# Softmax normalisation of a vision-transformer layer: whole-image Vector instructions, a third buffer, and a new order of the matmuls

## The chip, the core and the metric

The kernel runs on one core of one Trainium2 chip. The metric is the device time of one execution, in microseconds (us). It was timed three times before the change: 1443.85, 1444.19 and 1445.03 us.

Engines as the profile names them: PE is TensorE's matmuls, PEld its weight loads, DVE is VectorE, ACT is ScalarE, POOL is GpSimd, SP is SyncE, whose queue (SPq) here only issues DMAs.

## The reference

A patch embedding, one attention block with fake-quantised operands, and a gated feed-forward block with quantised weights. The change is in the attention block, of 64 images with 197 tokens, width 192, 12 heads of 64:

```python
def fake_quant(q, s, z):
    zr = ste_round(z)
    return s * (jnp.clip(ste_round(q / s) + zr, 0.0, 15.0) - zr)
...
qkv = fake_quant(x, sx1, zx1) @ fake_quant(ww1, sw1, zw1).T
q, k, v = map(split_heads, jnp.split(qkv, 3, axis=-1))
dots = jnp.einsum('bhnd,bhmd->bhnm', fake_quant(q, sq, zq), fake_quant(k, sk, zk)) * scale
a = jax.nn.softmax(dots, axis=-1)
out = jnp.einsum('bhnm,bhmd->bhnd', fake_quant(a, sa, za), fake_quant(v, sv, zv))
return fake_quant(out, sx2, zx2) @ fake_quant(ww2, sw2, zw2).T + bb2
```

So each image needs 12 score matrices of 197x197, their exponentials, the sum of each query's exponentials, a division, a rounding to int16, a clip to 0..15, and a product with the values.

## The kernel before

Three stages run one after the other: the embedding (18 packs of tiles, until some 230 us of the profiled span), the attention (one image after another, until some 1067 us) and the feed-forward (49 pairs of 128-row tiles and a rest). The engines are written out by hand, each in its own block, and meet through semaphores. Each engine works strictly in the order of its block; what orders the attention stage are `SLOTS` (the table of matmul pieces) and the order of the statements in each `image_step`.

**Layout.** Scores are kept transposed: keys on the partitions, queries along the free axis. The 197 keys of an image are two blocks, `TOK`: 128 keys and 69 keys (t = 0, 1). A unit u = 0..5 of an image is four heads (group g = u // 2) of one key block (t = u % 2): 4 x 197 = 788 columns.

**Pieces.** `image_step(b, par)` runs once per image b, with 6 slots. In slot u the tensor engine does the first piece of `SLOTS[u]`, then the scores of the next unit (L1149, four matmuls, called S below), then the sums of the unit before (L1161, called Z: a 32-column stationary operand with one non-zero column gathers the sum over keys of exp; four fp32 matmuls, recorded as eight), then the rest of the slot's pieces. The pieces, with the image that they serve as an offset to b:

- xt (L1093): transposes of the next image's input, which ACT copies to `xT` (L500)
- qk 0..5 (L1101): four matmuls each, which ACT rounds to `qki` (L504) and DVE clips to `qkb`, one clip for q and one for k
- v 0..3 (L1108): two matmuls each, rounded to `vi` by ACT (L513), clipped to `vb` by DVE
- o 0..2 (L1118, L1120): the product of probabilities and values of four heads, PV below: eight matmuls with 64 stationary columns, of which even heads write partitions 0 to 63 and odd heads 64 to 127; ACT rounds the result to `oi` (L525)
- y 0..1 (L1126): the output projection, from `ob`, which DVE clips from `oi`

Three PSUM banks (5, 6, 7) take the pieces in turn, so a piece waits until ACT has read the piece three places before it. Two pairs of banks take the scores, one pair for each t.

**Softmax.** ACT exponentiates a unit from PSUM into `ex` (L544), a ring of 12 units (2 images). When image b-1's last Z is done, DVE transposes the 12 x 197 sums (L877), takes reciprocals (L887) and transposes back to `zinv` (L906). SP writes them to DRAM in three DMAs (`z_row`, L415) and reads them back spread over all 128 partitions in three DMAs (`zb`, L420), one for each group of four heads, each with a semaphore of its own. DVE multiplies one unit of `ex` with its group of `zb` into int16 `pi` (L913, called TT below), 11 units behind the scores, and clips the unit to bf16 `pT` (L766 through `clip`, called clip P) one unit later:

```python
dve.wait_ge(s_zb[g], 16 * (image + 1))
dve.wait_ge(s_exp, U - TT_LAG + 1)
wait(dve, s_pb, U - TT_LAG - 1)
v.tensor_tensor(pi[0:r, t, :, 0:N], ex[0:r, w % U1 + U1 * ((par + w // U1) % 2), :, :], zb[0:r, g, :, :],
                ALU.mult).then_inc(s_pi, 1)
```

A PV piece of group k waits for both clips of its group, `pe.wait_ge(s_pb, 2 * G + 2)`.

Of the kernel before, what the change touches and what calls it, by code (L numbers as in the profile page):

```python
# [5 lines left out]
def vit_tower_kernel(nc, xt, w_tok, tok_b, cls_tok, w1t, w2t, bb2, quant, w_in_t, g_in, w_out_t, g_out,  # L6
# [10 lines left out]
    ALU = mybir.AluOpType  # L17
# [3 lines left out]
    B, N, D = out.shape  # L21
# [14 lines left out]
    with ctx:  # L36
# [42 lines left out]
        big = sb("big", [128, NR + NF + ND + PACK * KC * 128], fp32)  # L79
# [3 lines left out]
        xring = big[:, NR + NF + ND:].rearrange("p (a b) -> p a b", a=PACK)  # L83
        hb = sb("hb", [128, 2, PACK, D], fp32)
        hp = sb("hp", [128, 2, PACK, D], fp32)
# [5 lines left out]
        xi = sb("xi", [128, PACK, D], i16)  # L91
        xb = sb("xb", [128, 2, PACK, D], bf16)
# [3 lines left out]
        stage_i = sb("stage_i", [128, 2 * 3 * INNER], i16)  # L96
# [22 lines left out]
        pi = sb("pi", [128, 2, 4, N + 1], i16)  # L119
        pT = sb("pT", [128, 3, 2, 4, N + 1], bf16)  # L120
# [43 lines left out]
        s_zb = [sem(f"softmax_inverse_spread_{g}") for g in range(3)]  # L164
        s_zrow = [sem(f"softmax_inverse_stored_{g}") for g in range(3)]
# [119 lines left out]
        TT_LAG, CLIP_LAG = 11, 12  # L285
# [69 lines left out]
        def over_images(eng, step):  # L355


            for b in range(-1, 5):
                step(b, b % 2)
            with eng.Fori(0, (B - 8) // 2) as i:  # L360
                step(2 * i + 5, 1)
                step(2 * i + 6, 0)
            for b in range(B - 3, B + 3):
                step(b, b % 2)
# [10 lines left out]
        def _(sp):  # L375
# [29 lines left out]
            def image_step(b, par):  # L405
# [10 lines left out]
                if has_unit(b, -U1):  # L416
                    for g in range(3):
                        wait_apart(sp, s_zrow[g], 16 * b)
                        wait_apart(sp, s_pi, 6 * (b - 2) + 2 * g + 2)
                        sp.dma_start(zb[:, g, :, :].rearrange("p h n -> p (h n)"),  # L420
                                     z_row[g, :, :].rearrange("h n -> (h n)").partition_broadcast(128))\
                          .then_inc(s_zb[g], 16)
# [19 lines left out]
        def _(act):  # L442
# [92 lines left out]
            def image_step(b, par):  # L535
                n = 0
                for u in range(U1):
                    U = U1 * b + u
                    if exists(b, 0):
                        r = TOK[u % 2][1]  # L540
                        act.wait_ge(s_scores, U + 1)
                        wait(act, s_pi, U - 11)

                        act.activation(ex[0:r, U1 * par + u, :, :].rearrange("p (a h) n -> p a h n", a=2),  # L544
                                       psum[0:r, 2 * (u % 2):2 * (u % 2) + 2, 0:2 * N]
# [80 lines left out]
        def _(pool):  # L626
# [45 lines left out]
            def image_step(b, par):  # L672
# [44 lines left out]
        def _(dve):  # L717
# [555 lines left out]
```

## Time and profile before

| | us |
|---|---|
| median of 3 runs (lowest, highest) | 1444.19 (1443.85, 1445.03) |
| the profiled execution | 1445.15 |
| its span, first to last instruction | 1443.2 |
| DVE busy / PE busy / ACT busy in it | 1209.8 / 1218.4 / 990.7 |

The span is what the trace shows; the profiled execution's own time is 2.0 us longer than it. Busy time of PE is that of overlapping, modelled matmul records, so PE is read by the distance from the start of one group of matmuls to the start of the next, and by what it waited for.

### The profile page before, as it was taken

The numbers are of one execution on the slowest core, as the hardware profiler recorded it, in microseconds if no ns is written. First come the engines' busy times: TensorE is split into PE (matmuls) and PEld (weight loads), VectorE is DVE, ScalarE is ACT, GpSimd is POOL, SyncE is SP. The second block draws the span as 40 slices with busy tenths as digits, with TensorE's granted clock in tenths as the row PEclk, the third lists the DMA queues.
The fourth block names the chain that finished last, engine by engine and source line by source line (L and its number), as shares of the span: only waits on it lengthen the run. The fifth ranks groups of instructions, "written<-read, shape, count | busy, mean of one in ns | idle before, by whom it ended". The sixth has DMA issues, their size and how long they took to land.

```text
span 1443.2 us, 40676 instructions
## 1 busy us (share of the span) xinstructions
PE 1218.4 (84%) x11806; PEld 761.2 (53%) x11806; DVE 1209.8 (84%) x2868; ACT 990.7 (69%) x2005; POOL 457.1 (32%) x540
## 2 busy tenths in 40 slices
PE   5999992999999999999999999999846766767676
PEld 5999991445555555555555555555523333333343
DVE  4566782269999999999999999999978999999996
ACT  0000002568888888888888888888817888888886
POOL 7344541001111111111111111111126666666664
PEclk9999995569999999999999999999956787777765
DMA  6999972124444444444444444444532222222222
GB/s 246 267 281 276 299 246 64 44 76 117 119 120 120 120 120 120 120 120 120 120 119 121 120 119 119 117 120 117 126 75 61 83 82 82 82 82 86 83 73 69
DMA packets 142650, 182.38 MB, mean 126 GB/s; under 512 B 40528, under 2 KB 104784, under 8 KB 142288
## 3 DMA queue, kind: packets, MB, share of 16 engines
q1 hardware_dynamic: 71472, 134.72, 31.7%
q10 hardware_dynamic: 55776, 37.45, 8.8%
q0 software_dynamic: 15360, 9.70, 5.7%
q8 instruction: 20, 0.33, 0.1%
q14 instruction: 22, 0.18, 0.0%
HBM read 147.31 MB, written 34.50 MB: 126 GB/s over the span
## 4 chain that ended last, share of the span: by engine, by line
PE 74%; DVE 9%; issue 7%; ACT 5%; ACTq 2%; DMA 1%; DVEq 0%; SPq 0%; POOL 0%
PE psum L1044 13%; PE psum L1161 13%; PE psum L1101 12%; PE psum L1149 8%; PE psum L1108 7%; PE psum L1183 5%; PE psum L1126 5%; PE psum L1118 4%; PE psum L1120 2%; DVE big L1002 2%; ACT xT L500 2%; PE psum L1093 1%; PE psum L1204 1%; DVE oo L1019 1%; ACT big L574 1%
## 5 line engine op out<-in xcount | busy, mean ns | idle before, releaser
L913 DVE TENSOR_TENSOR pi<-big 128x788 int16<-128x788 f32 (+1 forms) x384 | 370.4, 965 | 0.0
L677 POOL DMA_DIRECT2D h_res<-att x128 | 118.1, 959 | 724.1 <-ACT att L520 722.4
L544 ACT ACTIVATE big<-psum 128x788 f32<-128x788 f32 (+1 forms) x384 | 314.8, 820 | 2.9 <-DVE pi L913 2.9
L1101 PE MATMUL psum<-xT,w1b 96*128 96x197 bf16 x1536 | 196.3, 259 | 43.3 <-ACT xT L500 43.3
L504 ACT ACTIVATE qki<-psum 128x394 int16<-128x394 f32 x384 | 179.1, 498 | 59.2 <-PE psum L1101 54.7
L1161 PE MATMUL psum<-big,sa_hot 128*32 128x197 f32 (+1 forms) x3072 | 216.0, 355 | 0.0
L1044 PE MATMUL psum<-big 128*128 128x192 f32 (+1 forms) x1200 | 197.3, 330 | 19.3 <-DMA big<-xt 17.3
L1044 PEld LDWEIGHTS psum<-big 128*128 128x128 f32 (+1 forms) x1200 | 195.4, 190 | 20.3 <-DVE big L722 17.2
L766 DVE TENSOR_SCALAR pT<-pi,lo,hi 128x788 bf16<-128x788 int16 (+1 forms) x384 | 185.3, 483 | 22.3
L1101 PEld LDWEIGHTS psum<-xT,w1b 96*128 96x128 bf16 x1536 | 124.6, 100 | 124.9 <-issue 65.8
L1183 PE MATMUL psum<-winb,zT 96*128 96x512 bf16 (+1 forms) x396 | 150.3, 548 | 34.8 <-DVE big L1002 34.2
L500 ACT ACT_TABLE_LOAD x1 | 1.3, 1283 | 238.6 <-issue 238.6
L1149 PE MATMUL psum<-qkb 64*128 64x197 bf16 (+1 forms) x1536 | 140.4, 263 | 2.6 <-DVE qkb L766 1.2
L766 DVE TENSOR_SCALAR qkb<-qki,lo,hi 128x1182 bf16<-128x1182 int16 x128 | 75.9, 593 | 77.9 <-ACT qki L504 77.9
L711 POOL TENSOR_TENSOR big<-big,goutb 128x512 f32<-128x512 f32 (+1 forms) x99 | 124.0, 1274 | 47.6 <-DVE big L1002 47.6
L513 ACT ACTIVATE vi<-psum 128x384 int16<-128x384 f32 (+1 forms) x256 | 117.9, 485 | 30.8 <-PE psum L1108 29.5
L1108 PE MATMUL psum<-w1b,xT 96*128 96x384 bf16 (+1 forms) x512 | 110.7, 341 | 0.0
L525 ACT ACTIVATE oi<-psum 128x394 int16<-128x394 f32 x192 | 97.2, 506 | 14.2 <-PE psum L1120 14.2
L1183 PEld LDWEIGHTS psum<-winb,zT 96*128 96x128 bf16 (+1 forms) x396 | 45.8, 126 | 113.1 <-issue 66.6
L1118 PE MATMUL psum<-pT,vb 128*64 128x197 bf16 x768 | 89.6, 264 | 12.4 <-issue 7.4
L1213 PE MATMUL psum<-woutb,yT 128*128 128x192 bf16 (+1 forms) x396 | 51.3, 285 | 56.7 <-ACT yT L566 56.7
L1161 PEld LDWEIGHTS psum<-big,sa_hot 128*32 128x32 f32 (+1 forms) x3072 | 61.7, 110 | 63.5 <-issue 26.5
(105 smaller groups left out, 1966.1 us busy)
## 6 DMA issues: line engine op xcount, KB each, us to landing
big<-z_row SPq DMA_DIRECT2D x192, 394.0 KB, 3.8
big<-xt SPq DMA_DIRECT2D x98, 384.0 KB, 4.3
tin<-h_res SPq DMA_DIRECT2D x49, 192.0 KB, 2.4
tres<-h_res ACTq DMA_DIRECT2D x49, 192.0 KB, 2.5
out<-oo ACTq DMA_DIRECT2D x49, 192.0 KB, 2.6
h_res<-hp ACTq DMA_DIRECT2D x96, 96.0 KB, 3.8
h_res<-att POOLq DMA_DIRECT2D x64, 96.0 KB, 3.5
x_int<-xb ACTq DMA_DIRECT2D x96, 48.0 KB, 3.9
```

The lines of the kernel that those rows point to most:

```text
L504: act.activation(qki[:, 2 * k:2 * k + 2, :], psum[:, bank, 0:2 * N] .rearrange("p (c n) -> p c n", c=2), ACT.Copy, scale=factor[F_Q if k < ...
L544: act.activation(ex[0:r, U1 * par + u, :, :].rearrange("p (a h) n -> p a h n", a=2), psum[0:r, 2 * (u % 2):2 * (u % 2) + 2, 0:2 * N] .rear ...
L711: g.tensor_tensor(yg[0:r, oth, a, :], yy[0:r, a, :], goutb[0:r, :], ALU.mult)\
L766: return v.tensor_scalar(dst, src, lo[0:r, which:which + 1], hi[0:r, which:which + 1], ALU.max, ALU.min)
L913: v.tensor_tensor(pi[0:r, t, :, 0:N], ex[0:r, w % U1 + U1 * ((par + w // U1) % 2), :, :], zb[0:r, g, :, :], ALU.mult).then_inc(s_pi, 1)
L1044: last = mm(psum[p0:p0 + r, s, 0:D], xring[:, s, c * 128 + p0:c * 128 + p0 + r], weight_of(cls, c), start=(c == 0), stop=(c == KC - 1))
L1101: last = mm(psum[:, bank, j * N:(j + 1) * N], w1b[:, c, ch:ch + 128], xT[:, c, :], start=(c == 0), stop=(c == 1))
L1108: last = mm(psum[0:r, bank, 0:W], xT[:, c, t0:t0 + r], w1b[:, c, 2 * INNER + half * W:2 * INNER + (half + 1) * W], start=(c == 0), stop=(c ...
L1118: mm(dst, vb[:, ip, 0, head * DH:(head + 1) * DH], pT[:, k, 0, j, 0:N], start=True, stop=False)
L1149: last = mm(psum[0:r, 2 * (w % 2) + i % 2, (i // 2) * N:(i // 2 + 1) * N], qkb[po:po + DH, ip, 6 + c, t0:t0 + r], qkb[po:po + DH, ip, c, 0:N],
L1161: last = mm(psum[32 * j:32 * j + 32, 4, 0:N], sa_hot[0:r, w // 2, :], ex[0:r, U1 * ip + w, j, :], start=(w == 0), stop=(w == 5))
L1183: last = mm(psum[0:r, 2 * a + half, :], zT3[:, oth, a, c, 0:r], winb[:, c, half * HID:(half + 1) * HID], start=(c == 0), stop=(c == 1))
```

## The change

1. **DVE works by key block.** One TT and one clip P per image and key block, over all 12 heads (2364 columns), so two of each per image in place of six of each. `pi`, `pT`, `zb` and `ex` are laid out for that: `ex` is a ring of three images, `zb` and `pT` hold two images, `vb` three. `zb` has one semaphore, and a TT waits for all three of its DMAs.
2. **A new order on DVE**, for image step b: clip `vb`, clip P of image b-3 block 1, the three small steps on the sums, TT of image b-2 block 0, clip q, clip P block 0, clip k, clip `ob`, TT of image b-2 block 1.
3. **A new `SLOTS`.** All PV pieces belong to image b-3 and stand first in slots 1, 2 and 3; the input transposes stand at the end of slot 0, and the first qk pieces come after the PV piece, S and Z of slot 1.
4. **PV matmuls alternate column halves** in program order: head 0 and head 1 for the first key block, then both for the second.
5. `hb`, `hp`, `xi`, `xb`, `stage_i` move into the shared buffer `big` (they are used only before the attention). The loop over images is unrolled six times instead of twice (9 rounds instead of 28).

The core of the diff:

```diff
-        ex = big[:, 0:NEX].rearrange("p (u h n) -> p u h n", u=12, h=4)
-        zb = big[:, NEX:NEX + 12 * N].rearrange("p (g h n) -> p g h n", g=3, h=4)
+        ex = big[:, 0:6 * HN].rearrange("p (i t h n) -> p i t h n", i=3, t=2, h=HEADS)
+        zb = big[:, 6 * HN:8 * HN].rearrange("p (i h n) -> p i h n", i=2, h=HEADS)
...
-        SLOTS = [[("v", 3, 0), ("o", 2, -3), ("xt", 0, 1)],
-                 [("qk", 0, 1), ("qk", 1, 1)],
-                 [("o", 0, -2), ("qk", 2, 1), ("v", 0, 1)],
-                 [("qk", 3, 1), ("qk", 4, 1), ("qk", 5, 1)],
-                 [("o", 1, -2), ("y", 0, -3)],
-                 [("y", 1, -3), ("v", 1, 1), ("v", 2, 1)]]
+        SLOTS = [[("v", 3, 0), ("xt", 0, 1)],
+                 [("o", 0, -3), ("qk", 0, 1), ("qk", 1, 1)],
+                 [("o", 1, -3), ("qk", 2, 1), ("qk", 3, 1)],
+                 [("o", 2, -3), ("qk", 4, 1), ("qk", 5, 1)],
+                 [("v", 0, 1), ("v", 1, 1)],
+                 [("v", 2, 1), ("y", 0, -3), ("y", 1, -3)]]
...
+                    wait_apart(sp, s_zb, 48 * (b - 1))
                     for g in range(3):
-                        wait_apart(sp, s_zb[g], 16 * (b - 1))
-                        sp.dma_start(z_row[g, :, :], zinv[g:128:32, 0:N]).then_inc(s_zrow[g], 16)
...
+                        sp.dma_start(z_row[g, :, :], zinv[g:128:32, 0:N]).then_inc(s_zrow, 16)
+                    wait_apart(sp, s_zrow, 48 * b)
+                    wait_apart(sp, s_pi, 2 * b - 4)
                     for g in range(3):
...
+                def clip_probs(image, ip, t):
+                    r = TOK[t][1]
+                    dve.wait_ge(s_pi, 2 * image + t + 1)
+                    wait(dve, full["o"], 3 * (image - 1))
+                    clip(pT[0:r, ip, t, :, 0:N], pi[0:r, t, :, 0:N], None, r, ZA).then_inc(s_pb, 1)
+
+                def normalise(image, ip, it, t):
+                    r = TOK[t][1]
+                    dve.wait_ge(s_zb, 48 * (image + 1))
+                    dve.wait_ge(s_exp, U1 * (image + 1))
+                    wait(dve, s_pb, 2 * image + t - 1)
+                    v.tensor_tensor(pi[0:r, t, :, 0:N], ex[0:r, it, t, :, :], zb[0:r, ip, :, :],
+                                    ALU.mult).then_inc(s_pi, 1)
...
-                    G = 3 * im + k
-                    pe.wait_ge(s_pb, 2 * G + 2)
+                    it = (tri + d) % 3
+                    pe.wait_ge(s_pb, 2 * im + 2)
                     pe.wait_ge(s_vb, im + 1)
...
+                    for c in range(2):
+                        for t, r in ((0, 128), (1, R1)):
+                            for i in range(2):
+                                head, j = 4 * k + 2 * c + i, 4 * k + ORD.index(2 * c + i)
+                                last = mm(psum[i * DH:(i + 1) * DH, bank, c * N:(c + 1) * N],
+                                          vb[0:r, it, t, head * DH:(head + 1) * DH], pT[0:r, ip, t, j, 0:N],
+                                          start=(t == 0), stop=(t == 1))
```

What it moves on DVE, in a steady image. Before, from the transpose of the sums on (L913 is TT, L766 with `pT` is clip P):

```order
L877 STREAM_TRANSPOSE zt<-psum 128x224
L766 TENSOR_SCALAR pT<-pi,lo,hi 69x4x197
L887 RECIPROCAL zti<-zt 128x7x3
...
L766 TENSOR_SCALAR vb<-vi,lo,hi 128x1536
L906 STREAM_TRANSPOSE zinv<-zti 128x224
...
L913 TENSOR_TENSOR pi<-big 128x4x197
...
L766 TENSOR_SCALAR pT<-pi,lo,hi 128x4x197
...
L913 TENSOR_TENSOR pi<-big 69x4x197
L766 TENSOR_SCALAR pT<-pi,lo,hi 69x4x197
```

Now, the whole image (L888 is TT, L771 with `big<-pi` is clip P, since `pT` lies in `big`):

```order
L771 TENSOR_SCALAR vb<-vi,lo,hi 128x1536
L771 TENSOR_SCALAR big<-pi,lo,hi 69x12x197
L906 STREAM_TRANSPOSE zt<-psum 128x224
L909 RECIPROCAL zti<-zt 128x7x3
L912 STREAM_TRANSPOSE zinv<-zti 128x224
L888 TENSOR_TENSOR pi<-big 128x12x197
L771 TENSOR_SCALAR qkb<-qki,lo,hi 128x6x197
L771 TENSOR_SCALAR big<-pi,lo,hi 128x12x197
L771 TENSOR_SCALAR qkb<-qki,lo,hi 128x6x197
L771 TENSOR_SCALAR ob<-oi,lo,hi 128x6x197
L888 TENSOR_TENSOR pi<-big 69x12x197
```

The second TT is now the last instruction of an image step, and its clip the second of the next one.

What it moves on PE, around the input transposes. Before, the first qk piece follows them directly:

```order
L1093 MATMUL psum<-ident,xq 96x69
L1101 MATMUL psum<-xT,w1b 128x197 [waits xt_read,v_read]
L1101 MATMUL psum<-xT,w1b 128x197 x3
L1149 MATMUL psum<-qkb 128x197 [waits exp_done]
L1149 MATMUL psum<-qkb 128x197 x3
L1161 MATMUL psum<-big,sa_hot 32x197 [waits softmax_sum_turned,exp_done]
L1161 MATMUL psum<-big,sa_hot 32x197 x3
```

Now (L1105 transposes, L1131 PV, L1161 S, L1173 Z, L1113 qk):

```order
L1105 MATMUL psum<-ident,xq 96x69
L1131 MATMUL psum<-big,vb 64x197 [waits v_quantised,probs_quantised,v_read]
L1131 MATMUL psum<-big,vb 64x197 x7
L1161 MATMUL psum<-qkb 128x197 [waits exp_done]
L1161 MATMUL psum<-qkb 128x197 x3
L1173 MATMUL psum<-big,sa_hot 32x197 [waits softmax_sum_turned,exp_done]
L1173 MATMUL psum<-big,sa_hot 32x197 x3
L1113 MATMUL psum<-xT,w1b 128x197 [waits xt_read,v_read]
L1113 MATMUL psum<-xT,w1b 128x197 x3
```

Between the transposes and the first qk piece there now stand a PV piece, S and Z, and that PV piece is the one that waits for the clip of the second key block.

## Rows read from the trace of the kernel before

**Rows 1.** The page: busy time, and the chain that ended last.

```profile
PE 1218.4 (84%) x11806; PEld 761.2 (53%) x11806; DVE 1209.8 (84%) x2868; ACT 990.7 (69%) x2005; POOL 457.1 (32%) x540
PE 74%; DVE 9%; issue 7%; ACT 5%; ACTq 2%; DMA 1%; DVEq 0%; SPq 0%; POOL 0%
```

**Rows 2.** Windows: length, busy PE, PEld, DVE, ACT, POOL; PEclk, DMA share, GB/s.

```profile
290.00:310.00 20.00, 19.32 (x149) 9.00 (x147) 12.76 (x22) 12.38 (x24) 0.00 (x0) 0.50 0.25 69
310.00:330.00 20.00, 19.25 (x209) 10.97 (x202) 14.61 (x25) 14.55 (x31) 3.14 (x4) 0.82 0.35 83
700.00:724.28 24.28, 22.83 (x291) 12.93 (x289) 22.41 (x40) 21.47 (x45) 3.70 (x4) 1.00 0.45 119
319.50:1023.40 703.90, 661.85 (x8356) 374.85 (x8353) 649.78 (x1103) 622.74 (x1277) 107.29 (x116) 1.00 0.48 119
```

**Rows 3.** Waits, 342.2 to 1023.4 us: waited in total, times, longest.

```profile
PE psum L1101 <- ACT xT L500: 37.8, 56, 0.8
DVE qkb L766 <- ACT qki L504: 25.7, 112, 0.4
```

**Rows 4.** Timeline of PE, one image: start us, us, what.

```profile
701.57 0.86 PE L1101 MATMUL psum<-xT,w1b 96*128 96x197 bf16 x8
...
707.86 0.39 PE L1093 MATMUL psum<-ident,xq 128*96 128x128 bf16 x4
708.93 0.52 PE L1101 MATMUL psum<-xT,w1b 96*128 96x197 bf16 x4 [0.68 <-ACT xT L500]
709.38 0.34 PE L1149 MATMUL psum<-qkb 64*128 64x197 bf16 x4
709.66 0.54 PE L1161 MATMUL psum<-big,sa_hot 128*32 128x197 f32 x8
710.13 0.52 PE L1101 MATMUL psum<-xT,w1b 96*128 96x197 bf16 x4
710.58 0.28 PE L1118 MATMUL psum<-pT,vb 128*64 128x197 bf16 x2
710.69 0.26 PE L1120 MATMUL psum<-pT,vb 69*64 69x197 bf16 x2
...
711.05 0.36 PE L1149 MATMUL psum<-qkb 64*69 64x197 bf16 x4
711.34 0.54 PE L1161 MATMUL psum<-big,sa_hot 69*32 69x197 f32 x8
```

**Rows 5.** Timeline of ACT, same stretch.

```profile
701.73 1.28 ACT L504 ACTIVATE qki<-psum 128x394 int16<-128x394 f32 x3
```

**Rows 6.** Timeline of DVE, same stretch.

```profile
703.05 0.59 DVE L766 TENSOR_SCALAR qkb<-qki,lo,hi 128x1182 bf16<-128x1182 int16 x1 [0.26 <-ACT qki L504]
703.55 0.97 DVE L913 TENSOR_TENSOR pi<-big 69x788 int16<-69x788 f32 x1
704.56 0.48 DVE L766 TENSOR_SCALAR pT<-pi,lo,hi 69x788 bf16<-69x788 int16 x1
...
707.53 0.42 DVE L877 STREAM_TRANSPOSE zt<-psum 128x224 f32<-128x224 f32 x1
...
708.43 0.57 DVE L766 TENSOR_SCALAR vb<-vi,lo,hi 128x1536 bf16<-128x1536 int16 x1
708.92 0.40 DVE L906 STREAM_TRANSPOSE zinv<-zti 128x224 f32<-128x224 f32 x1
```

**Rows 7.** Timeline of DVE before the attention: fp32 TENSOR_TENSOR of other lengths.

```profile
15.38 1.63 DVE L722 TENSOR_TENSOR big<-big 128x1152 f32<-128x1152 f32 x1
...
24.84 0.36 DVE L776 TENSOR_TENSOR hb<-psum,tokb 128x192 f32<-128x192 f32 x1 [0.42 <-PE psum L1044]
```

**Rows 8.** Timeline of SP's queue, same image: issues of the reciprocals' DMAs.

```profile
709.49 1.69 SPq L415 DMA_DIRECT2D z_row<-zinv  x3
```

**Rows 9.** The tensor `z_row`: its DMAs, and the time from issue to landing.

```profile
L420 SPq DMA_DIRECT2D big<-z_row x192: 319/330/448, 269.8 to 1052.7; - x192
DMA to landing us min/median/max: 3.4/3.8/5.3
```

More of the change, by code:

```diff
@@ L82, in vit_tower_kernel @@
         wmix = big[:, NR + NF:NR + NF + ND].rearrange("p (a b c) -> p a b c", a=2, b=2)
[L83 to L85 removed]
+        xring = big[:, o_x:o_h].rearrange("p (a b) -> p a b", a=PACK)
+        hb, hp = [big[:, o_h + k * NH:o_h + (k + 1) * NH].rearrange("p (a b c) -> p a b c", a=2, b=PACK)
+                  for k in range(2)]
         st = sb("st", [128, PACK, 6], fp32)
@@ L163, in vit_tower_kernel @@
         s_zinv = sem("softmax_inverse_ready")
-        s_zb = [sem(f"softmax_inverse_spread_{g}") for g in range(3)]
-        s_zrow = [sem(f"softmax_inverse_stored_{g}") for g in range(3)]
+        s_zb = sem("softmax_inverse_spread")
+        s_zrow = sem("softmax_inverse_stored")
         s_pi = sem("probs_int16_ready")
@@ L284, in vit_tower_kernel @@
         U1 = 6
-        TT_LAG, CLIP_LAG = 11, 12
         def has_unit(b, u):
@@ L358, in over_images @@
             for b in range(-1, 5):
[L359 to L364, printed above, removed]
+                step(b, b % 2, b % 3)
+            rounds = (B - 8) // 6
+            with eng.Fori(0, rounds) as i:
+                for j in range(6):
+                    step(6 * i + 5 + j, (5 + j) % 2, (5 + j) % 3)
+            for b in range(5 + 6 * rounds, B + 3):
+                step(b, b % 2, b % 3)
         def dst_rows(dram, y, x, half, along_x):
@@ new lines, in clip_qk @@
+                def clip_qk(half):
+                    dve.wait_ge(evac["qk"], 6 * (b + 1) + 3 * (half + 1))
+                    wait(dve, s_scores, 6 * b)
+                    clip(qkb[:, nxt, 6 * half:6 * half + 6, 0:N], qki[:, 6 * half:6 * half + 6, :], None,
+                         128, (ZQ, ZK)[half]).then_inc(s_qkb, 1)
+                if has_unit(b, -U1):
+                    dve.wait_ge(evac["v"], 4 * b)
+                    wait(dve, full["o"], 3 * (b - 3))
+                    clip(vb[:, (tri + 2) % 3, :, :], vi[:, nxt, :, :], None, 128, ZV).then_inc(s_vb, 1)
@@ new lines, in image_step @@
+                if has_unit(b, -3 * U1):
+                    clip_probs(b - 3, nxt, 1)
+                if has_unit(b, -U1):
+                    dve.wait_ge(s_zsum, b)
+                    wait(dve, s_zti, b - 1)
+                    v.transpose(zt[:, :, :].rearrange("p a b -> p (a b)"), psum[:, 4, 0:NZ]).then_inc(s_zt, 1)
+                    dve.wait_ge(s_zt, b)
+                    wait(dve, s_zinv, b - 1)
+                    v.reciprocal(zti[:, :, 0:3], zt[:, :, 0:3]).then_inc(s_zti, 1)
+                    dve.wait_ge(s_zti, b)
+                    wait(dve, s_zrow, 48 * (b - 1))
+                    v.transpose(zinv[:, :], zti[:, :, :].rearrange("p a b -> p (a b)")).then_inc(s_zinv, 1)
@@ new lines, in image_step @@
+                if has_unit(b, -2 * U1):
+                    normalise(b - 2, par, (tri + 1) % 3, 0)
+                if exists(b, 1):
+                    clip_qk(0)
+                if has_unit(b, -2 * U1):
+                    clip_probs(b - 2, par, 0)
+                if exists(b, 1):
+                    clip_qk(1)
+                if has_unit(b, -3 * U1):
+                    dve.wait_ge(evac["o"], 3 * b - 6)
+                    wait(dve, full["y"], 2 * b - 6)
+                    clip(ob[:, :, 0:N], oi[:, nxt, :, :], None, 128, ZX2).then_inc(s_ob, 1)
```

110 lines of the change are left out of this document (32 added, 78 removed).

## Prediction

> **What bounds the kernel now.** I read four views, from coarse to fine. The page's busy times and chain [rows 1] show PE and DVE both at 84% of the span, and PE on 74% of the chain that ended last. Neither says which of the two sets the pace, so the attention stage is read by itself. The windows [rows 2] show 703.90 us of it at a granted clock of 1.00 (2.4 GHz). One turn of the image loop, two images, is 24.28 us there, so an image takes 12.14 us and the stretch holds 703.90 / 12.14 = 58 images. In the turn DVE is busy 22.41 us and ACT 21.47 of 24.28.
>
> The waits [rows 3] name the pace: PE waits 56 times in 56 images for ACT's copy of the transposed input, 37.8 / 56 = 0.68 us each. DVE waits 112 times for ACT's rounding of q and k, 25.7 / 56 = 0.46 us per image, and ACT there waits for PE's products. So DVE follows PE with 0.46 us to spare, and PE is the bound. In the timeline of PE [rows 4] the reader is to see that groups start right behind each other (the next starts before the last one's modelled end), except at 708.93, where qk stands 1.07 us behind the transposes with 0.68 us idle.
>
> **What the groups cost, from start to next start** [rows 4]: a PV piece 711.05 - 710.58 = 0.47, S 0.28 (128 keys) or 0.29 (69 keys), Z 0.47, two qk pieces in a row 0.86 less the overlap of 0.07 = 0.79.
>
> **PE after the change.** Between transposes and the first qk piece now lie PV, S and Z: 0.47 + 0.28 + 0.47 = 1.22 us, more than the 0.68 waited. That wait leaves. Every piece is still there, and the switches between the shapes of group are as many as before, so PE's own need is 12.14 - 0.68 = 11.46 us an image.
>
> **DVE after the change.** TT: 788 elements take 0.97 us [rows 6], 192 take 0.36 [rows 7], so 0.61 / 596 = 1.02 ns an element, and 2364 take 0.97 + 1576 x 1.02 = 2.58; I take 2.61, since the shorter one reads PSUM and its slope may be a little low. Bounds: 2.58, and 3.34 at the rate of the other row of its kind (1152 in 1.63 us, beside adds of POOL) [rows 7]; three old ones would be 2.91. I take the low end because the 788-element row is this very instruction. Clip P: 788 take 0.48 and 1182 take 0.59 [rows 6], 0.27 ns an element, so 2364 take about 0.90. Bounds: 0.67 by the slope to the 1536-element clip (0.57), and three old ones, 1.45. By these, DVE saves per image 6 x 0.97 - 2 x 2.61 = 0.60 and 6 x 0.48 - 2 x 0.90 = 1.08 us, 1.7 together: it needs about 10 us an image and is far from being the bound by its sum. That saving is worth nothing in itself, since DVE already waited.
>
> **But the order closes a ring.** The first PV piece of step b waits for both clips of image b-3, and the second is the second DVE instruction of step b. In front of it on DVE stand, in order: clip k (which waits for ACT's reading of qk piece 5 of the step before), clip `ob`, the second TT, clip `vb`. And qk piece 5 stands behind that step's three PV pieces. So one image can't be shorter than this ring:
>
> - PE, start of PV 0 to end of qk 5: 3 PV 1.41, S 0.28 + 0.29 + 0.28, 3 Z 1.41, two qk pairs 1.58, and the third to its end 0.86: 6.11
> - ACT: qk ends at 701.57 + 0.86 = 702.43, its reading at 701.73 + 1.28 = 703.01 [rows 4, 5]: 0.58; and 0.04, since ACT is still reading qk 4 when qk 5 ends
> - to DVE 0.04 (703.05) [rows 6]
> - DVE: clip k to the next start 0.50 (703.05 to 703.55), clip `ob` (as many elements) the same 0.50, TT 2.61 less the 0.08 by which an independent instruction starts early = 2.53, clip `vb` 0.49 (708.43 to 708.92), clip P whole 0.90: 4.92
> - back to PE 0.07 (an estimate, of the size of the 0.04 from ACT to DVE)
>
> The sum is 11.76 us. It is above PE's 11.46, so the ring binds, and PE stands 0.3 us before the first PV piece. The gain is 12.14 - 11.76 = 0.38 us an image, over 58 images 22.0 us.
>
> **The rest.** Four images before 319.5 us run at a clock of 0.50 (1.2 GHz) and 96% busy PE [rows 2]; groups are longer there and DVE is only 64% busy, so PE binds and 0.68 leaves each time: 2.7 us. The third image of `ex` and of `vb` only frees waits that did not occur. The DMAs of the reciprocals stay six per image (three stores, three reads), but all three reads now wait for all three stores. Stores start 0.17 behind `zinv` (708.92 + 0.40) and are issued by 711.18 [rows 6, 8]; with an estimated 1.5 to land, then three issues of 0.33 and up to 5.3 for the reads to land [rows 9], they are there some 9.7 us behind `zinv`, and the first TT needs them 11.4 behind: hidden, with 2 us of cover; without that cover each us would go into every image. The transpose of the sums now stands behind clip P on DVE, ending 0.4 us after it; the Z that waits for it starts 0.75 after the PV piece: hidden by 0.3 us. At the end, last TTs and clips are shorter in sum, but PV of the last image can't start until all 12 heads are clipped: I count 0, with 2 us either way. Embedding and feed-forward are untouched. A longer program: no row shows an engine waiting for code in the loop; I count 0.
>
> **PV in alternating halves.** The rows show PV matmuls in couples: two of L1118 within 710.58 to 710.86, then from 710.69 two of L1120, though the program of before writes L1118, L1120, L1118, L1120 [rows 4]. So the two column halves already run side by side, 8 matmuls in four steps, and the new order gives nothing. The Trainium skill's page "TensorE: Matmul & The Clock Gate" (Part 3, "The mechanism") says otherwise, that matmuls start and end strictly in program order. That is a rival below.
>
> **The sum.** 1445.15 (the profiled execution, 0.96 above the median) - 22.0 - 2.7 = 1420.4; I say 1420. Its own range comes from the ring's parts, from 1409 (clip P at its low bound, 0.2 us less an image) to 1436 (a TT of 2.91).
>
> **Rivals.**
>
> *The ring is not tight* (0.13). If the clips come out at their low bound (0.23 less) and the hand-overs a little shorter, PE binds at 11.46: 0.68 x 58 + 2.7 = 42 us, 1403. For it: my hand-overs are summed without slack. Against: the ring would have to be 0.3 shorter.
>
> *Program order decided on PE* (0.04). If matmuls ran in program order, the old PV took five steps and the new one four. A step is 710.69 - 710.58 = 0.11 us, and three pieces lie in the ring: 0.33 an image, 19 us more, 1401. Against it stand the couples of [rows 4], in which the trace disagrees with the page.
>
> *The ring is longer than the old image, and it is slower* (0.11). The two whole-image instructions stand in the middle of the ring, where the old ones of 0.97 and 0.48 us could be placed between waits. From 0.38 us more in it than I summed, the change loses. At the rate of the 1152-element row a TT is 3.34: ring 12.49, 0.35 x 58 = +20 - 2.7, so 1463. If clip P fell to three old ones, 12.31: 1452. For it: a ring of five hand-overs collects every delay. Against: the same instructions run here at 0.97 with the same operands in the same memory.
>
> *The change doesn't do what it says* (0.10): a whole-image TT costs as much as three old ones, 2.91, since its time goes by elements alone. Ring 11.76 + 0.30 = 12.06, and 1445.15 - 0.08 x 58 - 2.7 = 1438. Against: 192 and 788 elements differ by 1.02 ns each, which leaves 0.17 us that is paid once per instruction. Part of this case lies within what can't be told from no change.
>
> *The clock.* The granted clock is 0.50 until 310 us and 0.82 on the mean of 310 to 330 [rows 2], so it rises near 317, some images into the attention, when PV is already running; PV now begins one image later. At 0.50 PE needs up to half as long again for an image, so one more there costs about 6 us and one fewer gives as much (an estimate). That moves the forecast to 1426 or 1414, inside its own range, so it has no chance of its own.
>
> **How the numbers follow.** The forecast has 0.62. The range 1398 to 1438 takes in PE's floor and the case without saving, and leaves out the slower rival and edges. A measurement of this kernel can tell about 0.2%, 3 us. Faster by more than that: 0.62 + 0.13 + 0.04 + most of 0.10 = 0.86; within it 0.03; slower 0.11.
>
> **What would show it.** An image of 11.76 us in the loop; PE's wait before the first qk piece gone, and a new one of about 0.3 us before the first PV piece, released by DVE's clip P; TT at 2.6 and clip P at 0.9 us; DVE idle about 1.1 us per image before clip k, waiting for ACT's `qki`; PV still 0.47. I am wrong if an image is under 11.5 or over 12.1, if PE waits for the transposed sums or DVE for `zb`, or if PV takes less than 0.45.

## The result and the profile after

The changed kernel takes 1514.04 us (median of 4 runs, 1508.20 to 1516.95), the kernel before in runs beside it 1444.02 (1443.13 to 1445.03). The ratio is 1.048, 95% interval 1.0446 to 1.0513: slower by 70 us, where 24 us less was forecast and the range ended at 1438. The profiled execution took 1512.75 us.

The page of the changed kernel answers to [rows 1]: busy time, the granted clock in 40 slices, the queue that brings instructions, and the two new groups.

```profile
PE 1288.2 (85%) x11806; PEld 788.5 (52%) x11806; DVE 1131.4 (75%) x2356; ACT 995.5 (66%) x2005; POOL 475.4 (31%) x540
...
PEclk9999995589898897979797979889965777777875
...
q8 instruction: 99, 1.62, 0.4%
...
L888 DVE TENSOR_TENSOR pi<-big 128x2364 int16<-128x2364 f32 (+1 forms) x128 | 332.6, 2598 | 2.2 <-DMA big<-z_row 2.0
...
L771 DVE TENSOR_SCALAR big<-pi,lo,hi 128x2364 bf16<-128x2364 int16 (+1 forms) x128 | 114.5, 894 | 0.2
```

DVE's part came out as costed: a TT takes 2.60 us (2.61 forecast), a clip P 0.89 (0.90), and DVE is busy 78 us less than before. PE runs the same 11806 matmuls and is busy 70 us *more*. The clock row says why: in the attention its digits go up and down between 9 and 7, where a granted clock of 1.00 throughout was expected. The last hint is q8, which brings instructions: 99 packets. The same row of the page of before, which the prediction does not use:

```profile
q8 instruction: 20, 0.33, 0.1%
```

The windows answer to [rows 2]: a plain image, then the image that holds the jump back of the loop, the one behind it, the next one, and the whole stretch of 58 images (columns as there).

```profile
351.60:363.40 11.80, 11.41 (x148) 6.42 (x144) 9.93 (x12) 10.70 (x24) 2.21 (x3) 1.00 0.50 126
...
387.00:402.40 15.40, 11.93 (x149) 6.44 (x145) 10.82 (x12) 11.39 (x24) 4.04 (x4) 0.98 0.48 109
402.40:420.60 18.20, 18.20 (x148) 9.44 (x145) 10.04 (x11) 10.83 (x22) 0.36 (x1) 0.55 0.20 72
420.60:431.90 11.30, 11.30 (x149) 6.39 (x145) 9.30 (x11) 10.67 (x24) 2.01 (x3) 1.00 0.51 130
316.50:1087.00 770.50, 729.12 (x8357) 401.48 (x8353) 577.86 (x638) 627.00 (x1276) 125.21 (x116) 0.90 0.43 111
```

A plain image takes 11.80 us; 11.76 was forecast. But two images in each turn of six are long, 15.4 and 18.2 us here, and the second of them runs at a granted clock near 0.50 (1.2 GHz) with as many matmuls as any other. This happens eight times, once at each jump back of a loop of nine rounds.

The timeline of PE over one jump: start us, us, what. The `y` piece at 396.47 is the last of the turn, the `v` piece at 400.89 the first of the next.

```profile
387.03 0.39 PE L1105 MATMUL psum<-ident,xq 128*96 128x128 bf16 x4
387.82 0.54 PE L1131 MATMUL psum<-big,vb 128*64 128x197 bf16 x8 [0.40 <-DVE big L771]
388.29 0.35 PE L1161 MATMUL psum<-qkb 64*128 64x197 bf16 x4
...
396.47 1.35 PE L1138 MATMUL psum<-w2b,ob 128*128 128x192 bf16 x12
400.89 0.51 PE L1120 MATMUL psum<-w1b,xT 96*69 96x384 bf16 x2 [3.08 <-issue]
...
404.13 0.89 PE L1173 MATMUL psum<-big,sa_hot 128*32 128x197 f32 x8
```

The timeline of DVE in the same image, around clip q (392.15) and clip k (394.56):

```profile
392.15 0.60 DVE L771 TENSOR_SCALAR qkb<-qki,lo,hi 128x1182 bf16<-128x1182 int16 x1 [0.44 <-ACT qki L509]
...
394.56 0.59 DVE L771 TENSOR_SCALAR qkb<-qki,lo,hi 128x1182 bf16<-128x1182 int16 x1 [1.00 <-ACT qki L509]
```

At 387.82 stands the new wait that was forecast, 0.40 us before the first PV piece, released by clip P, and DVE idles 1.00 us before clip k as the ring wants it. At 400.89 PE stands 3.08 us, and no semaphore or transfer of the kernel releases it: "issue". Soon after, the same eight Z matmuls take 0.89 us that take 0.54 in [rows 4]. PE's waits from 342 to 1000 us answer to [rows 3]:

```profile
PE psum L1120 <- issue: 24.8, 8, 3.3
PE psum L1131 <- DVE big L771: 12.6, 32, 0.4
```

Eight such stops, 24.8 / 8 = 3.1 us each, and the wait for `xT` is gone. The queue of instructions over one turn (402.6 to 484.1 us), in the view of the DMAs:

```profile
q8 instruction: 9, 0.15, 0.7%
```

Nine packets of 16 KB in each turn: the loop's code is fetched again every time. In the loop of before, two images long, the same view has no such line from 356 to 1012 us. One of the nine packets lies inside PE's stop, which lasts from 397.82 to 400.89 us. The same view of the changed kernel from 398 to 399 us:

```profile
q8 instruction: 1, 0.02, 6.4%
```

So the loss has two parts. The kernel with a turn of four images (second section of the experiments) takes 686.5 us for these 58 images and the changed kernel 770.50: 84.0 us more, 10.5 per jump, of which 3.1 are PE standing and 7.4 are left for the time at half clock. Of the 89.6 us between the two profiled runs the rest, 5.6 us, lies outside this stretch.

### The profile page after: what moved, and what is told of

Same layout as the page of the kernel before. It is cut to its first block, busy times and chain, and to the rows that moved or that the text cites. A ratio compares the mean times of both kernels' runs of the same rounds, so it can differ in the third digit from the quotient of the medians.

```text
span 1510.7 us, 38086 instructions
## 1 busy us (share of the span) xinstructions
PE 1288.2 (85%) x11806; PEld 788.5 (52%) x11806; DVE 1131.4 (75%) x2356; ACT 995.5 (66%) x2005; POOL 475.4 (31%) x540
## 4 chain that ended last, share of the span: by engine, by line
PE 49%; DVE 19%; DMA 12%; issue 12%; ACT 3%; SPq 2%; ACTq 1%; DVEq 1%; POOL 0%
PE psum L1056 12%; PE psum L1173 7%; PE psum L1113 7%; DMA big<-z_row 7%; DVE pi L888 7%; PE psum L1195 5%; PE psum L1161 4%; PE psum L1131 4%; PE psum L1120 4%; DMA z_row<-zinv 3%; PE psum L1138 2%; DVE big L1014 2%; SPq L421 2%; DMA big<-xt 2%; DVE big L771 2%
## 5 line engine op out<-in xcount | busy, mean ns | idle before, releaser
L682 POOL DMA_DIRECT2D h_res<-att x128 | 137.1, 1321 | 770.4 <-ACT att L525 770.3
L888 DVE TENSOR_TENSOR pi<-big 128x2364 int16<-128x2364 f32 (+1 forms) x128 | 332.6, 2598 | 2.2 <-DMA big<-z_row 2.0
L1173 PE MATMUL psum<-big,sa_hot 128*32 128x197 f32 (+1 forms) x3072 | 232.2, 378 | 0.0
L771 DVE TENSOR_SCALAR qkb<-qki,lo,hi 128x1182 bf16<-128x1182 int16 x128 | 75.9, 593 | 185.2 <-ACT qki L509 185.2
L1113 PE MATMUL psum<-xT,w1b 96*128 96x197 bf16 x1536 | 190.5, 274 | 0.6 <-ACT xT L505 0.6
L1113 PEld LDWEIGHTS psum<-xT,w1b 96*128 96x128 bf16 x1536 | 136.7, 106 | 75.3 <-issue 66.4
L1120 PE MATMUL psum<-w1b,xT 96*128 96x384 bf16 (+1 forms) x512 | 133.9, 370 | 24.8 <-issue 24.8
L1161 PE MATMUL psum<-qkb 64*128 64x197 bf16 (+1 forms) x1536 | 149.6, 278 | 0.0
L1131 PE MATMUL psum<-big,vb 128*64 128x197 bf16 (+1 forms) x1536 | 115.3, 277 | 26.3 <-DVE big L771 15.2
L771 DVE TENSOR_SCALAR big<-pi,lo,hi 128x2364 bf16<-128x2364 int16 (+1 forms) x128 | 114.5, 894 | 0.2
L1161 PEld LDWEIGHTS psum<-qkb 64*128 64x128 bf16 (+1 forms) x1536 | 52.4, 106 | 104.9 <-issue 102.7
L1173 PEld LDWEIGHTS psum<-big,sa_hot 128*32 128x32 f32 (+1 forms) x3072 | 63.4, 113 | 70.4 <-issue 47.4
```

Of the source, the lines that this page charges most:

```text
L682: pool.dma_start(h_res[bass.ds(b - 3, 1), t0:t0 + r, :].rearrange("a n d -> (a n) d"), att[0:r, nxt, t, :], accum_op=ALU.add).then_inc(s_a ...
L771: return v.tensor_scalar(dst, src, lo[0:r, which:which + 1], hi[0:r, which:which + 1], ALU.max, ALU.min)
L888: v.tensor_tensor(pi[0:r, t, :, 0:N], ex[0:r, it, t, :, :], zb[0:r, ip, :, :], ALU.mult).then_inc(s_pi, 1)
L1113: last = mm(psum[:, bank, j * N:(j + 1) * N], w1b[:, c, ch:ch + 128], xT[:, c, :], start=(c == 0), stop=(c == 1))
L1120: last = mm(psum[0:r, bank, 0:W], xT[:, c, t0:t0 + r], w1b[:, c, 2 * INNER + half * W:2 * INNER + (half + 1) * W], start=(c == 0), stop=(c ...
L1131: last = mm(psum[i * DH:(i + 1) * DH, bank, c * N:(c + 1) * N], vb[0:r, it, t, head * DH:(head + 1) * DH], pT[0:r, ip, t, j, 0:N], start=( ...
```

## The experiments

Theory F: a six-image turn doesn't stay at hand, the fetch stops PE at the jump, and the stop costs the clock. Rival D: the new DVE order, or the third buffer, makes the long images. The experiments ran on three chips, each beside the kernel before: 1447.22 us on the first (long loop, written out, four-image turn, clip `vb` moved), 1448.13 on the second (one DMA, two DMAs, split instructions, old PV order), 1444.57 on the third (the other two stops, and the last version).

### The long loop in the kernel before

The loop of the kernel before is written six images long and nothing else is touched.

```diff
-            with eng.Fori(0, (B - 8) // 2) as i:
-                step(2 * i + 5, 1)
-                step(2 * i + 6, 0)
-            for b in range(B - 3, B + 3):
+            rounds = (B - 8) // 6
+            with eng.Fori(0, rounds) as i:
+                for j in range(6):
+                    step(6 * i + 5 + j, (5 + j) % 2)
+            for b in range(5 + 6 * rounds, B + 3):
```

> The kernel before with one edit: the image loop holds six images in place of two (9 turns). Theory F (code: at the jump back PE's program for six images is no longer at hand, PE idles some 3 us until it is fetched, and the granted clock then falls to 0.50 for some 20 us): in the trace of the change a turn of six images costs 82.0 us and its five undisturbed images 11.80 each would make 70.8, so 11.2 us a turn; over 8 jumps 1444 + 90 = 1534 us. Theory D (the stall belongs to the new order of pieces or to a DMA that it waits for): 1444 us, no stall.

Measured: 1545.62 us (1544.09 to 1546.28), ratio 1.0681 (1.066 to 1.0702). Its instruction queue, then PE's waits from 342 to 1000 us:

```profile
q8 instruction: 99, 1.62, 0.4%
```

```profile
PE psum L1102 <- ACT xT L501: 31.7, 47, 0.7
PE psum L1109 <- issue: 30.7, 7, 4.9
```

Same 99 packets, the same kind of stop at each jump (the eighth lies behind this window), and the old 0.7 us wait for `xT` still there. 1534 was expected by F and no change by D, so D falls: the loop alone costs 98.4 us, 12.3 per jump, of it 30.7 / 7 = 4.4 standing, with nothing of the change on DVE or in the order of PE. F had put the stop at some 3 us; why it is longer in this kernel than in the changed one is not shown.

### The change without the long loop

Two ways. In one, all 68 image steps are written out:

```diff
-            for b in range(-1, 5):
-                step(b, b % 2, b % 3)
-            rounds = (B - 8) // 6
-            with eng.Fori(0, rounds) as i:
-                for j in range(6):
-                    step(6 * i + 5 + j, (5 + j) % 2, (5 + j) % 3)
-            for b in range(5 + 6 * rounds, B + 3):
+            for b in range(-1, B + 3):
```

> The change without its loop: all 68 image steps written out one after the other. Theory F: no jump, no stall; 58 images at 11.8 us make 1421 us, clock 1.00 throughout the attention. A rival of F, P (it is the amount of code that hurts, PE's program being fetched all the time): slower than 1514 us, with gaps spread over all images. Theory D: 1514 us, one stall in six images.

In the other the rings of `ex` and `vb` have four places, so that four images close a turn (some tiles of the feed-forward move into `big` for room):

```diff
-        vb = sb("vb", [128, 3, 2, INNER], bf16)
+        vb = sb("vb", [128, 4, 2, INNER], bf16)
...
-        ex = big[:, 0:6 * HN].rearrange("p (i t h n) -> p i t h n", i=3, t=2, h=HEADS)
+        ex = big[:, 0:8 * HN].rearrange("p (i t h n) -> p i t h n", i=4, t=2, h=HEADS)
...
-                for j in range(6):
-                    step(6 * i + 5 + j, (5 + j) % 2, (5 + j) % 3)
+                for j in range(4):
+                    step(4 * i + 5 + j, (5 + j) % 2, (5 + j) % 4)
...
```

> The change with rings of four (exponentials, values) in place of three, so that the loop holds four images (14 turns). Theory F: some 98 KB of PE's program per turn (147 KB of fetched code per turn of six in the change's trace); if that is kept as the two images of before are, 1421 us without a stall; if it is not, 13 stalls of 11 us, 1565 us. Theory D: a stall in every sixth image or none at all by the ring, 1514 or less, not tied to the jump.

Measured: written out 1428.77 us (1426.75 to 1430.92), ratio 0.9877 (0.9854 to 0.99); four images a turn 1424.34 (1421.24 to 1426.76), ratio 0.9847 (0.9822 to 0.9873). Windows of the first, then its instruction queue:

```profile
340.00:1000.00 660.00, 634.03 (x8006) 359.31 (x8002) 552.87 (x610) 597.43 (x1222) 106.53 (x110) 1.00 0.48 124
```

```profile
q8 instruction: 82, 1.34, 0.4%
```

And of the second its 58 images, PE's wait from 342 to 1000 us, and its queue:

```profile
313.40:999.90 686.50, 661.89 (x8357) 372.53 (x8353) 576.02 (x638) 621.15 (x1277) 129.45 (x117) 1.00 0.48 122
```

```profile
PE psum L1131 <- DVE big L771: 23.2, 54, 0.5
```

```profile
q8 instruction: 22, 0.36, 0.1%
```

The written-out kernel fetches 82 packets and does not lose the clock in this stretch: fetching straight ahead is hidden, and only the jump costs. The four-image turn is not fetched again (from 380 to 990 us its view of the DMAs has no q8 line), and this is the kernel that was forecast (1421 was expected of both): 23 us less than before, an image of 686.5 / 58 = 11.84 us. By the packets, six images are 9 x 16 = some 150 KB of code (so four are about 100, two about 50), which came back each turn; a loop of two or four did not.

The Trainium skill's page "Runtime: NRT & Kernel Launch" (section "Instruction fetch mechanics") gives PE 128 KiB for instructions, filled in blocks of 16 KiB and sequentially ahead, and says that a taken branch to code outside the current window of two such blocks stalls until it is fetched. On the stall the trace agrees: nine packets of 16 KB a turn and 3.1 us at the jump with six images. On the two blocks it does not: turns of some 50 and 100 KB jumped back without a packet and without a stop. The three lengths go with the 128 KiB instead (50 and 100 KB stayed at hand, 150 did not); no run has a length between 100 and 150 KB.

### What does a stop of PE cost by itself?

Theory C: any stop of this kind costs the clock, whatever causes it. The four-image kernel gets a stop of PE at the top of each turn, released by a small DMA, with no fetch in the loop. It comes 14 times in a run. Which piece of PE the DMA's issue waits for sets how long PE stands. The edit for one DMA behind the last `y` piece (its two semaphores and the small tile it fills are left out):

```diff
             def image_step(b, par, tri):
+                if tri == 0 and (not isinstance(b, int) or 8 <= b <= 60):
+                    wait_apart(sp, full["y"], 2 * (b - 3))
+                    for k in range(1):
+                        if k:
+                            wait_apart(sp, s_gap[0], 4 * b - 16)
+                        sp.dma_start(gap_t[:, :], quant.partition_broadcast(128)).then_inc(s_gap[k], 16)
...
             def image_step(b, par, tri):
+                if tri == 0 and (not isinstance(b, int) or 8 <= b <= 60):
+                    pe.wait_ge(s_gap[0], 4 * b - 16)
```

> The kernel with rings of four (1424 us, no stall), with a pause put in once per four images: at the start of the step PE waits for one small DMA that SP issues when the last product of the step before is read out to be done (the last y piece). Some 2 us of idle PE, 14 times. Theory C (an idle PE of a few us is enough for the granted clock to fall to 0.50 for some 20 us, which costs more than the pause): if 2 us are enough, 14 x (2 + 8) = +140 us, 1564; if not, 14 x 2 = +28, 1452 us at a clock of 1.00. Rival (the clock fell because of the jump or the code fetched, not the idle time): 1452 us.

Two DMAs in a row:

```diff
-                    for k in range(1):
+                    for k in range(2):
...
-                    pe.wait_ge(s_gap[0], 4 * b - 16)
+                    pe.wait_ge(s_gap[1], 4 * b - 16)
```

> As the one before, with two such DMAs one after the other: some 4 us of idle PE, longer than the 3.1 us of the change's trace. Theory C: the clock falls behind every pause, 14 x (4 + 8) = +168 us, 1592 us. Rival (jump or fetch): 14 x 4 = +56 us, 1480 us, clock 1.00.

One DMA, issued one `y` piece earlier:

```diff
-                    wait_apart(sp, full["y"], 2 * (b - 3))
+                    wait_apart(sp, full["y"], 2 * (b - 3) - 1)
```

> The kernel with rings of four and one pause in four images as before (2.73 us of idle PE made the clock fall each time), its DMA issued one y piece earlier: some 2.2 us idle. Theory C with the same fall: 14 x (1.7 + 8) = 1560 us; if 2.2 us is short enough for the clock to stay at 1.00: 1424 + 14 x 2 = 1452 us.

One DMA, issued at the last `v` piece:

```diff
-                    wait_apart(sp, full["y"], 2 * (b - 3))
+                    wait_apart(sp, full["v"], 4 * b + 3)
```

> The same with the DMA issued at the last v piece of the step before, some 1.9 us before its end: some 0.9 us idle, of which the wait in front of the first PV piece gives back some 0.4. The kernel that splits the DVE instructions stands 0.9 us in every image at a clock of 1.00, so no fall: 1424 + 14 x 0.5 = 1431 us. If a pause in this place makes the clock fall whatever its length, 1424 + 14 x 8.5 = 1543 us.

Measured, one run each: 1565.55, 1602.84, 1546.77 and 1432.38 us, where 1564, 1592, 1560 or 1452, and 1431 were expected. The waits of each, in this order, whole span:

```profile
PE psum L1128 <- DMA gap_t<-quant: 38.4, 14, 2.9
```

```profile
PE psum L1128 <- DMA gap_t<-quant: 76.8, 14, 5.7
```

```profile
PE psum L1128 <- DMA gap_t<-quant: 29.2, 14, 2.7
```

```profile
PE psum L1128 <- DMA gap_t<-quant: 10.6, 14, 1.1
```

Windows from the third (stops of 2.1 us), before, behind and well behind a stop, and of the fourth (0.8 us) over its attention:

```profile
400.00:415.00 15.00, 14.60 (x192) 8.45 (x189) 12.19 (x14) 13.87 (x30) 2.31 (x2) 1.00 0.44 107
422.00:439.00 17.00, 17.00 (x133) 8.62 (x131) 9.93 (x11) 9.66 (x19) 0.00 (x0) 0.51 0.26 83
445.00:470.00 25.00, 24.14 (x311) 13.45 (x309) 20.72 (x24) 22.74 (x47) 4.51 (x4) 1.00 0.48 116
```

```profile
314.00:1030.00 716.00, 682.63 (x8610) 382.58 (x8608) 596.86 (x658) 640.00 (x1311) 135.31 (x122) 1.00 0.47 121
```

In the third kernel one stop of the 14 did not lower the clock: the last, 2.1 us long, ended at 1098.49 us. The stretch behind it:

```profile
1099.00:1122.80 23.80, 23.36 (x300) 13.11 (x300) 19.16 (x22) 21.45 (x44) 3.43 (x5) 1.00 0.47 119
```

Against the four-image kernel's time (1424.3; for one DMA and two DMAs 1425.8, that of its twin on their chip, in the last experiment), divided by the stops. The last column is what is lost beyond the standing, for each time that the clock fell, worked out before rounding. The long loop of the first experiment stands beside them, against the kernel before:

| kernel | PE stands, us | lost per stop, us | clock fell | beyond the stop, us |
|---|---|---|---|---|
| one DMA at the last `v` | 0.8 | 0.6 | 0 of 14 | none |
| one DMA, a `y` piece earlier | 2.1 | 8.7 | 13 of 14 | 7.2 |
| one DMA | 2.7 | 10.0 | 14 of 14 | 7.2 |
| the changed kernel, its jump | 3.1 | 10.5 | 8 of 8 | 7.4 |
| the kernel before with the long loop | 4.4 | 12.3 | 8 of 8 | 7.9 |
| two DMAs | 5.5 | 12.6 | 14 of 14 | 7.2 |

The changed kernel's loss is that of a stop of PE of its length, whoever causes it. Of the 58 stops of 2.0 us or more in this table, 57 brought the clock down to 1.2 GHz, for 14 to 24 us, at 7 to 8 us whatever the stop's length. The 14 shortest (0.7 to 0.9 us, the first 1.15) never did. Between 1.15 and 2.0 us these kernels have no such stop.

The length of a single stop is not all that decides. In the feed-forward of the kernel before, where PE stands again and again, the granted clock is 0.73 on the mean, although the longest stop in this window is 1.2 us:

```profile
1120.00:1165.00 45.00, 33.26 (x180) 17.59 (x179) 44.00 (x149) 38.67 (x79) 28.62 (x39) 0.73 0.30 84
```

### Is the ring what sets the 11.8 us?

Three edits of the four-image kernel. First, clip `vb` goes from the front of the DVE step behind the transpose back to `zinv`. It is then ahead of TT block 0 and no longer between the second TT and clip P, so the ring loses its 0.6 us (start to next start in the changed kernel; 0.49 in the prediction's sum) and PE should bind.

```diff
-                if has_unit(b, -U1):
-                    dve.wait_ge(evac["v"], 4 * b)
-                    wait(dve, full["o"], 3 * (b - 3))
-                    clip(vb[:, (tri + 3) % 4, :, :], vi[:, nxt, :, :], None, 128, ZV).then_inc(s_vb, 1)
                 if has_unit(b, -3 * U1):
...
                     v.transpose(zinv[:, :], zti[:, :, :].rearrange("p a b -> p (a b)")).then_inc(s_zinv, 1)
+                if has_unit(b, -U1):
+                    dve.wait_ge(evac["v"], 4 * b)
+                    wait(dve, full["o"], 3 * (b - 3))
+                    clip(vb[:, (tri + 3) % 4, :, :], vi[:, nxt, :, :], None, 128, ZV).then_inc(s_vb, 1)
```

> As the kernel with rings of four, and DVE clips the values behind the reciprocals in place of ahead of the second clip of probabilities. Ring theory (PE's first PV piece waits for the chain clip k, clip ob, TT, clip vb, clip P): the ring loses the 0.5 us of clip vb, an image falls from 11.80 to PE's own 11.4 to 11.5 us, 58 x 0.35 = 20 us less than the kernel with rings of four (1401 if that is 1421). Rival (PE binds, the wait in front of PV is slack that comes back elsewhere): no difference, 11.80.

Measured: 1399.50 us (1394.72 to 1400.29), ratio 0.9676 (0.9658 to 0.9695), 24.8 less than without the edit. Four images in its windows:

```profile
710.00:755.60 45.60, 45.48 (x577) 25.72 (x576) 40.11 (x45) 42.78 (x89) 7.42 (x8) 1.00 0.51 127
```

An image is 11.40 us, and PE has no wait for clip P left. The ring was the bound, and one clip of 0.6 us in it was worth 25 us, with DVE doing the same work as without the edit.

Second, TT and clip P are each split into three instructions of 788 columns, order and semaphores kept:

```diff
-                    clip(pT[0:r, ip, t, :, 0:N], pi[0:r, t, :, 0:N], None, r, ZA).then_inc(s_pb, 1)
+                    for g in range(3):
+                        ins = clip(pT[0:r, ip, t, 4 * g:4 * g + 4, 0:N], pi[0:r, t, 4 * g:4 * g + 4, 0:N], None, r, ZA)
+                    ins.then_inc(s_pb, 1)
...
-                    v.tensor_tensor(pi[0:r, t, :, 0:N], ex[0:r, it, t, :, :], zb[0:r, ip, :, :],
-                                    ALU.mult).then_inc(s_pi, 1)
+                    for g in range(3):
+                        h = slice(4 * g, 4 * g + 4)
+                        ins = v.tensor_tensor(pi[0:r, t, h, 0:N], ex[0:r, it, t, h, :], zb[0:r, ip, h, :], ALU.mult)
+                    ins.then_inc(s_pi, 1)
```

> The kernel with rings of four, with each whole-image TT and clip P written as three instructions of 788 columns again, in the same places and with the same waits; all else as there. Ring theory: in the ring TT grows from 2.53 to about 3 x 0.89 = 2.67 (0.97 less the overlap of 0.08) and clip P from 0.90 to 0.40 x 2 + 0.48 = 1.28, 0.52 us more, 11.85 -> 12.37 us an image, 58 x 0.52 = 30 us slower than the kernel with rings of four, 1454. Rival (the merging is hidden, the gain comes from the new order of the pieces alone): 1424 us.

Measured: 1467.33 us (1461.18 to 1475.97), ratio 1.0142 (1.0091 to 1.0193). The timeline of DVE, three instructions to a row, and PE's wait from 342 to 1020 us:

```profile
700.08 2.75 DVE L892 TENSOR_TENSOR pi<-big 69x788 int16<-69x788 f32 x3
702.75 0.67 DVE L771 TENSOR_SCALAR vb<-vi,lo,hi 128x1536 bf16<-128x1536 int16 x1
703.33 1.27 DVE L771 TENSOR_SCALAR big<-pi,lo,hi 69x788 bf16<-69x788 int16 x3
```

```profile
PE psum L1135 <- DVE big L771: 50.1, 53, 1.0
```

In the ring that is 2.75 - 2.61 = 0.14 and 1.27 - 0.89 = 0.38 more, 0.52, and the image went from 11.84 to 12.36 (four of them took 49.45 us from 703.36 us on), or 0.52. So the merged instructions do matter, by half a microsecond an image, since they lie in the ring (the same split of the other key block, outside it, added nothing): it costs 58 x 0.52 = 30 us of the 43 by which this kernel is slower than the four-image kernel. In the profiled run another 6 us are one early image of 19.64 us, less 1.0 that the next one gave back. In it the granted clock was 0.50:

```profile
341.00:358.00 17.00, 17.00 (x128) 8.82 (x120) 9.95 (x16) 9.65 (x20) 1.29 (x2) 0.50 0.23 79
```

It fell just behind the second of PE's waits of 1.0 us for clip P. It did not fall behind the first, nor behind the more than 50 of 0.9 to 1.0 us that followed in the loop. So a stop of this length can come with a fall, and mostly does not; what made the difference is not shown. Of the remaining 7 us 5.5 lie behind the last image's transposes, and they are not explained.

Third, on top of the first edit, the `y` pieces are set apart and clip `ob` goes ahead of clip k:

```diff
-                if exists(b, 1):
-                    clip_qk(1)
                 if has_unit(b, -3 * U1):
...
                     clip(ob[:, :, 0:N], oi[:, nxt, :, :], None, 128, ZX2).then_inc(s_ob, 1)
+                if exists(b, 1):
+                    clip_qk(1)
...
-                 [("v", 2, 1), ("y", 0, -3), ("y", 1, -3)]]
+                 [("y", 0, -3), ("v", 2, 1), ("y", 1, -3)]]
```

> The kernel with rings of four and clip vb behind the reciprocals (1399.5 us), with the last piece of v between the two y pieces (they follow it, and the second y waits some 0.2 us until ACT has read that v piece out of their common bank), and clip ob ahead of clip k on DVE so that the first y is not late. If PE is the bound there: 0.17 to 0.2 us an image, 58 x 0.18 = 10 us faster, 1389. Rival: ACT, busy 94% there, becomes the bound and the gain is 0 to 4 us.

Measured: 1386.18 us (1383.54 to 1388.51; 1389 was expected), ratio 0.9594 (0.9563 to 0.9624). Windows of four images, and DVE's largest wait, 342 to 980 us:

```profile
700.00:744.72 44.72, 44.72 (x578) 25.67 (x577) 41.00 (x45) 42.80 (x89) 8.27 (x8) 1.00 0.48 130
```

```profile
DVE qkb L771 <- ACT qki L509: 13.4, 59, 0.3
```

An image is 11.18 us and PE never stands. This is the fastest of all, 58 us under the kernel before on its chip. Two edits went in together, and their shares were not separated.

### Do alternating PV matmuls give anything?

The four-image kernel with the old order, head by head:

```diff
-                        for t, r in ((0, 128), (1, R1)):
-                            for i in range(2):
+                        for i in range(2):
+                            for t, r in ((0, 128), (1, R1)):
```

> The kernel with rings of four, its PV matmuls back in the old program order (both key blocks of a head, then the next head). Theory of the prediction (the two column halves already run side by side in either order): 11.85 us an image as with the new order, PV 0.47 us from start to next start, no difference in time. Rival (matmuls start in program order): PV takes five steps of 0.09 to 0.11 in place of four, all three pieces lie in the ring, 0.3 us an image, 58 x 0.3 = 17 us slower than the kernel with rings of four.

Measured: 1425.77 us (1422.00 to 1428.14), ratio 0.9841 (0.9812 to 0.987), beside 0.9847 for its twin. The same piece, in PE's timeline with the old order:

```profile
699.80 0.54 PE L1131 MATMUL psum<-big,vb 128*64 128x197 bf16 x8
700.28 0.35 PE L1161 MATMUL psum<-qkb 64*128 64x197 bf16 x4
```

From start to next start it is 0.48 us, and 388.29 - 387.82 = 0.47 in the changed kernel: no difference.

## Why the prediction was wrong

**The step that failed** is one sentence: "A longer program: no row shows an engine waiting for code in the loop; I count 0." A loop of two images can't show what a loop of six will wait for; the absence of a row was taken for a cost of nothing, and no upper bound was given. The page did have a row that bears on it: 20 packets on q8 in a program that makes 28 turns, so the loop's code was not brought anew each turn. That should have raised the question up to what length this holds. The runs put in its place 8 x 10.5 = 84 us, of which 8 x 3.1 = 25 is PE waiting for code and 59 the clock.

Even with a term for the fetch alone I would have said 1445, about no change. The larger part is the clock, and [rows 2] held its price: at 0.50 the same work takes PE up to half as long again.

**What held:**
- The ring: 11.80 us an image against 11.76 summed, and the two experiments on it moved it by about what stood in the sum (0.44 for clip `vb`, 0.52 for the split). Of its terms, TT 2.60 (2.61) and clip P 0.89 (0.90); clip `vb` took 0.59 from its start to the next (0.49). Of the signs named, the wait before the first PV piece was 0.40 (0.3), and DVE idle 1.00 before clip k (1.1).
- The saving as a total, without the long loop: the four-image kernel has a ratio of 0.9847, which is 22 us under 1444.02; the terms were 22.0 + 2.7. That the total fits so well is in part luck. In the profiled runs its 58 images gave 703.90 - 686.50 = 17.4 us, not 22.0, and the five image steps ahead of them 5.6, not 2.7.
- No wait for `xT` in the loop; no wait of PE for the transposed sums; `zb` in time but for 2.0 us in the whole program.
- PV in alternating halves gives nothing. The rival by strict program order on PE, which would have been worth 19 us, falls with the last experiment, as [rows 4] had said.

**What was off in size.** PE's own need was put at 11.46 us an image; with the ring out of the way PE took 11.40 in one order of pieces and 11.18 in another. The rival "ring not tight" would thus have been cheaper than 1403. And four half-clock images gained more than their 2.7: most of their transposes start 15.28 us apart in the changed kernel and 16.16 or 18.4 before, and the first five images together took 74.5 us there against 79.5. One bound of the prediction's own range is a slip: with a TT of 2.91 its sum gives 1438, as in the rival of that price, and not 1436.

**The rivals.** The slower side had 0.11, and all of it stood on a longer ring. The ring was not longer; the way in which it turned out slower had no rival of its own, though the unrolling stood in the change as its last line.

## What to carry to other kernels

Cost the length of a loop's body as a part of the change: look at what the instruction queue brings per turn before and after, and if the new body might not stay at hand, either write the loop shorter (here by a ring whose length divides it, four places in place of three) or write it out. Where PE is the bound, price a stop of PE by its length *and* by the clock behind it: here a stop of 2.0 us or more cost 7 to 8 us on top, in 57 cases of 58. And an instruction's duration is worth something where it lies in the ring of waits that closes each turn, and nothing elsewhere: read the order first, then the busy time.

## What was not expected of the hardware

- Code fetched straight ahead, 82 packets in the written-out kernel, cost some 4 us (1428.8 against 1424.3), while nine packets a turn with a jump back cost 84.
- A stop of 0.7 us in every image of the kernel before, and of 0.8 in every turn of one experiment, left the clock alone, and so did nearly all of 0.9 to 1.0 us in every image of another; stops of 2.1, 2.7, 3.1, 4.4 and 5.5 us (means) lowered it 57 times out of 58, for 14 to 24 us, and the price was 7 to 8 us whatever their length.
- Three 788-column instructions with no wait between them take 2.75 us as TT and 1.27 as clips, so merging saves 0.14 and 0.38 us, less than three times the single rows of before had it (0.97 x 3 - 2.61 = 0.30 and 0.48 x 3 - 0.89 = 0.55): they overlap at their ends.
